# Second expert routing: sends to HBM two tiles at a place instead of four, routing steps moved to other places, and the first pass of maxima reduced two PSUM banks at a time

## The reference, cut to what matters

```python
x = L0_attn_x                                   # (8, 512, 128)
xn = _layernorm(x, axis=-1)
s = _L0_attn_ref(xn, ...)                       # two small attentions, a Holt filter, norms, a feed forward
g = _silu(_L0_ffn_ref(xn, Wg, w1, w2))          # top-1 of 16 experts
x = x + s * g
xn = _layernorm(x, axis=-1)
s = _L1_attn_ref(xn, Wq, Wk, Wv, Wo)            # causal, 16 heads, ALiBi
g = _silu(_L1_ffn_ref(xn, gate_w, gate_b, ...)) # top-2 of 8 experts
x = x + s * g
```

```python
logits = xt @ gate_w.T + gate_b
top_v, top_i = jax.lax.top_k(logits, TOP_K)     # TOP_K = 2, E = 8
w = jax.nn.softmax(top_v, axis=-1)
out = (w * sel).sum(axis=1)
```

## Time and profile before

| what | value |
|---|---|
| runs | 1189.53, 1193.96, 4205.56 us (median 1193.96) |
| the profiled execution's own time | 1191.96 us |
| its span | 1190.1 us |
| busy share of the span | PE 85%, VectorE 67%, ScalarE 54%, POOL 49% |
| mean granted TensorE clock | 0.92 |

### The profile page before, as it was taken

The page is one execution under the profiler, slowest core; times in us unless marked ns, Lnnn a source line. Parts: engine busy times, 40 slices in busy tenths (PEclk is TensorE's granted clock), DMA queues, the critical chain, the costliest instruction groups (busy, mean ns, idle before and its releaser), DMA issues. The chain is left out here.

```text
span 1190.1 us, 22919 instructions
## 1 busy us (share of the span) xinstructions
PE 1013.1 (85%) x7466; PEld 543.2 (46%) x7466; DVE 791.7 (67%) x2466; ACT 646.8 (54%) x1252; POOL 578.1 (49%) x670
## 2 busy tenths in 40 slices
PE   4878899999989898878788577777999899899797
PEld 2612279433434333323333244444889654445443
DVE  5597833678787888887765555765444477788641
ACT  1204732576667776656566344444444466677575
POOL 5276400337464655547677576743000155545564
PEclk8667999999999999988999787877999999999889
DMA  5853566733223232303324033233888644454321
GB/s 144 217 146 80 136 169 200 223 102 91 54 56 88 46 98 47 89 5 87 82 66 98 12 74 92 50 85 115 241 242 252 162 108 111 83 135 110 68 56 45
DMA packets 121864, 129.81 MB, mean 109 GB/s; under 512 B 13920, under 2 KB 104864, under 8 KB 121536
## 3 DMA queue, kind: packets, MB, share of 16 engines
q1 hardware_dynamic: 115184, 115.37, 37.4%
q0 software_dynamic: 6144, 12.60, 4.0%
q10 hardware_dynamic: 432, 0.52, 0.2%
HBM read 82.54 MB, written 52.35 MB: 113 GB/s over the span
## 5 line engine op out<-in xcount | busy, mean ns | idle before, releaser
L877 DVE TENSOR_REDUCE a_neg_max<-ps_banks 128x1 f32<-128x512 f32 x512 | 322.7, 681 | 74.5 <-PE ps_banks L590 66.4
L772 ACT ACTIVATE a_probs<-ps_banks 128x512 f32<-128x512 f32 x512 | 278.3, 599 | 143.1 <-PE ps_banks L583 138.4
L583 PE MATMUL ps_banks<-q_strip,k_strip 53*128 53x512 bf16 (+3 forms) x1024 | 281.0, 355 | 72.1 <-DVE a_neg_max L877 31.5
L590 PE MATMUL ps_banks<-k_strip,q_strip 51*128 51x512 bf16 (+3 forms) x1024 | 301.5, 363 | 24.5 <-DVE a_neg_max L883 11.8
L883 DVE CUSTOM_DVE_ANT_0 a_masked<-ps_banks,mask_wide 128x384 bf16<-128x384 f32 (+3 forms) x512 | 224.0, 487 | 90.3 <-PE ps_banks L590 74.6
L774 ACT ACTIVATE a_probs<-ps_banks 128x512 f32<-128x512 f32 x256 | 144.2, 600 | 81.2 <-PE ps_banks L541 72.1
L1067 POOL DMA_INDIRECT tokens<-made,at x96 | 93.6, 975 | 175.6 <-DMA made<-work 124.8
L583 PEld LDWEIGHTS ps_banks<-q_strip,k_strip 53*128 53x128 bf16 x1024 | 72.2, 95 | 161.9 <-issue 54.4
L624 PE MATMUL ps_banks<-a_probs,v_aug 128*32 128x512 f32 x1024 | 141.4, 625 | 0.5 <-ACT a_o_strip L779 0.2
L590 PEld LDWEIGHTS ps_banks<-k_strip,q_strip 51*128 51x128 bf16 x1024 | 74.4, 95 | 142.9 <-ACT a_probs L772 58.7
L2000 POOL DMA_INDIRECT sent<-xn,at x64 | 62.6, 978 | 54.7 <-DMA sent<-xn,at 24.4
(11 more groups left out here) (258 smaller groups left out, 1709.0 us busy)
## 6 DMA issues: line engine op xcount, KB each, us to landing
work<-in_pack SPq DMA_DIRECT2D x39, 450.0 KB, 3.5
q_rows<-a_q_parts SPq DMA_DIRECT2D x96, 128.0 KB
k_rows<-a_k_parts SPq DMA_DIRECT2D x96, 128.0 KB
q_strip<-q_rows SPq DMA_DIRECT2D x64, 192.0 KB
k_strip<-k_rows SPq DMA_DIRECT2D x64, 192.0 KB
work<-in_w SPq DMA_DIRECT2D x32, 256.0 KB, 3.1
sent<-in_zeros SPq DMA_DIRECT2D x14, 512.0 KB, 8.1
work<-sent SPq DMA_DIRECT2D x55, 128.0 KB, 3.3
```

Source lines behind the costliest of these rows:

```text
L583: mm = pe.matmul(sbank[:, at:at + hi - lo], k_now[rows(js, ROW_END), slot, kt * P:(kt + 1) * P], q_now[rows(js, ROW_END), slot, lo:hi], st ...
L590: mm = pe.matmul(mbank[:, at:at + hi - lo], q_next[rows(jm, ROW_SHIFT), slot, qt * P:(qt + 1) * P], k_next[rows(jm, ROW_SHIFT), slot, lo:h ...
L772: act.activation(probs[si // 4 % 2][:, si % 4, :], bank, ACT.Exp).then_inc(sems["probs"], 1)
L877: dve.tensor_reduce(neg_max[:, half, qt, hd:hd + 1], bank, AX.X, ALU.max, negate=True).then_inc(sems["max_out"], 1)
```

## The change

Four things are changed. (1) `routed` takes the three places of the ends as a list, so they can stand apart. (2) Group 0 in stage 5 gets its steps earlier and further apart: choose at 12, 14, 16, 18 (was 13, 15, 18, 21), count and scan at 20 (was 25), ends at 22, 24, 25 (was 27, 28, 29), slots at 27 (was 30), weights at 29 (was 28). (3) The sends stand two tiles at a place: at 0, 15, 19 and 24 of stage 6 (tiles 0 to 7), at 0, 14, 18 and 25 of stage 7 (8 to 15), at 0, 7, 17 and 23 of stage 8 (16 to 23), at 4 and 10 of stage 9 (24 to 27), and the last four tiles at 18 of stage 9 as before. The count of sends is unchanged: stages 6, 7, 8 and 9 have 8, 8, 8 and 8 tiles, where they had 12, 8, 4 and 8. (4) In the pass of maxima VectorE waits for two banks and reduces them in one instruction of 2 x 512 columns, and TensorE may be one pair ahead of what is reduced (`ahead = 2`, the four banks taken as two pairs).

```diff
 def routed(g, choose, count, ends, slots, weigh, table):
...
-                  *({ends + part: [("place", 0, (g, 1, part))]} for part in range(3)), {slots: [("place", 0, (g, 2))]}, {weigh: [("weigh", 0, g)]}, {table: [("place", 0, (g, 3))]})
+                  *({end: [("place", 0, (g, 1, part))]} for part, end in enumerate(ends)), {slots: [("place", 0, (g, 2))]}, {weigh: [("weigh", 0, g)]}, {table: [("place", 0, (g, 3))]})
...
-    NB - 2: sends(0, *4 * (0,), *4 * (13,), *4 * (30,)),
-    NB - 1: merged(routed(1, (12, 13, 15, 16), 18, 20, 23, 24, 26), sends(12, *4 * (17,), *4 * (30,))),
...
+    NB - 2: sends(0, *2 * (0,), *2 * (15,), *2 * (19,), *2 * (24,)),
+    NB - 1: merged(routed(1, (12, 13, 15, 16), 18, (20, 21, 22), 23, 24, 26), sends(8, *2 * (0,), *2 * (14,), *2 * (18,), *2 * (25,))),
...
+def paired(arg):
+
+    return arg[1] is not None and arg[0] is None
...
-        return {**({"scores": 1, "probs": 1} if arg[0] is not None else {}), **({"max_in": 1, "max_out": 1} if arg[1] is not None else {})}
+        return {**({"scores": 1, "probs": 1} if arg[0] is not None else {}), **({"max_in": 1, "max_out": 2 * (arg[1] % 2) if paired(arg) else 1} if arg[1] is not None else {})}
...
-                                mbank, ahead = banks[:, 2 + n.at("max_in") % 4, :], 3
+                                mbank, ahead = banks[:, 2 + n.at("max_in") % 4, :], 2
...
+                            if paired(arg):
+
+                                if mi % 2 == 1:
+                                    wait(dve, sems["max_in"], n.at("max_in") + 1)
+                                    both = banks[:, 1 + n.at("max_in") % 4:3 + n.at("max_in") % 4, :]
+                                    dve.tensor_reduce(neg_max[:, half, qt, QT + slot % QT::-QT], both, AX.X, ALU.max, negate=True).then_inc(sems["max_out"], 2)
+                            elif max_layer == 0:
```

More of the change, by code:

```diff
@@ L201 @@
     2: {24: [("masks", 0)]},
-    NB - 3: routed(0, (13, 15, 18, 21), 25, 27, 30, 28, 31),
-    NB - 2: sends(0, *4 * (0,), *4 * (13,), *4 * (30,)),
-    NB - 1: merged(routed(1, (12, 13, 15, 16), 18, 20, 23, 24, 26), sends(12, *4 * (17,), *4 * (30,))),
-    NB: merged(routed(2, (13, 14, 15, 16), 17, 20, 25, 26, 27), sends(20, *4 * (18,))),
-    ROUTE1: merged(routed(3, (8, 9, 10, 11), 13, 15, 18, 19, 21), sends(24, *4 * (4,)), sends(28, *4 * (18,))),
+    NB - 3: routed(0, (12, 14, 16, 18), 20, (22, 24, 25), 27, 29, 31),
+    NB - 2: sends(0, *2 * (0,), *2 * (15,), *2 * (19,), *2 * (24,)),
+    NB - 1: merged(routed(1, (12, 13, 15, 16), 18, (20, 21, 22), 23, 24, 26), sends(8, *2 * (0,), *2 * (14,), *2 * (18,), *2 * (25,))),
+    NB: merged(routed(2, (13, 14, 15, 16), 17, (20, 21, 22), 25, 26, 27), sends(16, *2 * (0,), *2 * (7,), *2 * (17,), *2 * (23,))),
+    ROUTE1: merged(routed(3, (8, 9, 10, 11), 13, (15, 16, 17), 18, 19, 21), sends(24, *2 * (4,), *2 * (10,)), sends(28, *4 * (18,))),
     **{MIX1 + i: mixed(-2, 8, 0, 18, 22, 24, 26, 28) for i in range(4)},
@@ L870, in _ @@
                             _, mi, max_layer = arg
-                            bank = banks[:, 2 + n.at("max_in") % 4 if b == -1 else MAX_BANK + n.at("max_in") % RING, :]
+                            bank = banks[:, MAX_BANK + n.at("max_in") % RING, :]
                             half, j, pieces = max_unit(mi, max_layer)
@@ L874, in _ @@
                             hd, e = QT * j + slot % QT, mi % 10
-                            wait(dve, sems["max_in"], n.at("max_in") + 1)
-                            if max_layer == 0:
+                            if paired(arg):
[4 more added lines that the diff above has]
+                            elif max_layer == 0:
+                                wait(dve, sems["max_in"], n.at("max_in") + 1)
                                 dve.tensor_reduce(neg_max[:, half, qt, hd:hd + 1], bank, AX.X, ALU.max, negate=True).then_inc(sems["max_out"], 1)
                             else:
+                                wait(dve, sems["max_in"], n.at("max_in") + 1)
                                 wait(dve, sems["max_out"], n.at("max_out") - 1)
```

## The result

| kernel | runs (us) | median |
|---|---|---|
| before | 1193.96, 1189.53, 4205.56, 1194.90 | 1194.43 |
| changed | 1175.42, 1177.87, 1176.26, 1170.73 | 1175.84 |

The ratio is 0.9851, with a 95% interval from 0.9802 to 0.9900 (the run at 4205.56 is left out of it). So some 18 us are gained: the interval is clear of no change and ends just short of a gain of 2%. The profiled executions are 1191.96 and 1175.42 us, 16.5 us apart.

A forecast was written before the change was run, and what follows sets the result against it. POOL's queue, with sends ahead of the scan of stage 7, was taken as the limit there. From 1191.96 us, -12.8 (stages 6 and 7), -4.9 (stage 8), -1.5 (stage 5) and -1.0 (maxima) gave 1172 us, range 1162 to 1186.

The forecast's parts named there:

- the forecast case: POOL's queue still sets the scan of stage 7: 1172 us, own range 1166 to 1178, chance 0.50.
- Stages 6 and 7: Fewer sends ahead on POOL: `ln3a` 5.9 us earlier plus 6.9 us ahead of the scan, gain 12.8 us.
- the second case: Rival: VectorE's wait in stage 7 goes altogether, by an earlier gather or rows landing sooner; 1165 us, chance 0.24.
- x2 at stage 7, 0.8 us late and covered: VectorE waits 0.8 us for x2 at the `ln3a`, which its three banks in hand cover.
- Stage 8: TensorE's 4.76 us wait to turn xn goes; net of delays and with a clock gain, 4.9 us less.
- the sign of being wrong: VectorE waiting over 3 us for x2 at the head of stage 7 or 8; 1 to 3 us was expected.
- the sends ahead of `ln2`: Sends at place 25 of stage 7 fall in POOL's 4.72 us idle time and cost about 2 us.
- both delays: In stage 8, later x2 and later y, from sends between the splits of q and k: 1.4 us charged together.
- the 1.5 us by clock: Stage 8, at mean clock 0.82, gains 1.5 us from a higher clock, out of 0 to 10.
- Stage 5: Group 0's routing moves from the stage's end to its middle: 1.5 us less, from -3.5 to +1.5.
- Pass of maxima: Reducing two banks at once, 1.12 us a pair against 1.20: 1.0 us less, from -2.5 to +4.
- The slower rival: Sends ahead of `ln2` in stages 6, 7 and 8 delay x2 by 6.8 us each: 1197.5 us, chance 0.06.

The follow-up runs named there:

- sends: The kernel before with only the new places of the sends in stages 6 to 9: 1150.4 us against 1175.4, ratio 0.9781.
- scan: The kernel before with two of the four tiles at place 17 of stage 7 sent at 21, behind the scan: 1189.8 us against 1195.1, ratio 0.9957.
- head: The kernel before with two of the four tiles at place 30 of stage 6 sent at 24, ahead of `ln2`: 1191.1 us against 1195.1, ratio 0.9973.
- after_b: The changed kernel, unchanged, timed again in the third group of runs: 1150.7 us against 1178.1 for the kernel before, ratio 0.9776.
- pairs: The kernel before with only the maxima reduced in pairs of banks: 1175.6 us against 1175.4, ratio 0.9993.
- after_again: The changed kernel, unchanged, timed again in the second group of runs: 1177.3 us against 1195.1 for the kernel before, ratio 0.9837.
- before_again: The kernel before, unchanged, timed again beside itself in the second group of runs: 1196.4 us against 1195.1, ratio 1.0008.
- late: The changed kernel without the sends at place 25 of stage 7, later tiles following two later each: 1154.9 us against 1178.1 for the kernel before, ratio 0.9802.
- group0: The kernel before with only group 0's steps in stage 5 at their new places: 1178.0 us against 1175.4, ratio 1.0023.
- single: The changed kernel with maxima reduced one bank at a time again, three banks ahead: 1149.9 us against 1175.4 for the kernel before, ratio 0.9782.
- single_b: The changed kernel with single-bank maxima again, repeated in the third group of runs: 1149.5 us against 1178.1 for the kernel before, ratio 0.9770.
- x2late: The changed kernel with two tiles moved from place 0 of stage 7 to place 24 of stage 6: 1157.3 us against 1178.1 for the kernel before, ratio 0.9839.

## Why the prediction was right, and where it was not

The forecast of 1172 us was 3.8 us under the median, and the mechanism is the one forecast: POOL's queue sets the scan of stage 7, and moving DMAs out from ahead of it shortens that stage. `sends` and `scan` show it in time and trace with one edit each, `head` in its trace alone. That the sum came out so near is in part luck. In the first pair of traces stages 5 to 8 are 20.2 us shorter, just the sum forecast, but only because the terms that missed made up for each other; the second pair has 17.0 us there, and `after_b` against `pairs` 27.3. And where the kernel before takes 1178 us (`after_b`, below), the same change gains 26 to 27 us, at the far end of the 14 to 26 that the 1166 to 1178 of the forecast case mean.

- **Stages 6 and 7: -12.8 forecast, -16.9 measured** in the first pair of traces, -16.3 in the second (134.8 in `after_again`, 151.1 in `before_again`). The steps on POOL came as worked out: the gate 2.6 us earlier (forecast 2.4), the `ln3a` 6.3 (5.9). The mis-sized term is the end of the scan, 16.2 instead of 12.8 earlier. I had kept the 5.12 us wait for the gathered rows and named its shortening only under the second case. It fell by 3.3 us, nearly all of the 3.4 that were missing, and left 1.15 us of VectorE's wait instead of 4. `head` shows the same fall (1.81), `scan` doesn't (4.92): it goes with the head start of the gather. Stage 7 also got its clock back: 0.91 before, 1.00 after, TensorE's busy time 58.76 and 56.52 us. I had put the gain in clock to stage 8.
- **x2 at stage 7, 0.8 us late and covered:** VectorE waits 0 us for it in the first trace and 1.6 in `after_again` and `after_b`. That is within the 1.8 us of three banks.
- **Stage 8: -4.9 forecast, -0.9 and -1.0 measured** on the chips of the first comparison and of `after_again`, but -6.7 in `after_b` against `pairs`, two traces of the other kind of chip (below). The wait to turn xn is gone, as forecast. In its place came what I named as the sign of being wrong, a wait of over 3 us for x2 (3.75 us, 4.0 in `after_again`, 3.8 in `after_b`). The step that failed here: I charged the sends ahead of `ln2` with 2 us, which is their 6.8 less the 4.72 us that POOL was idle there. But POOL waited there for VectorE's moments, and VectorE came late in part because the scan had held it for 14.53 us. With the scan early this cover shrinks: `late`, which has no sends there, is left with 2.59 us of it. The four sends take 5.35 us, and no landing is waited for, so `ln2` starts 3.0 us after the moments are there, and VectorE's wait for x2 grows by the same 3.0 (0.72 to 3.75). The larger part of the miss is in two other terms. I charged both delays with 1.4 us; TensorE's waits for maxima in stage 8 alone went from 5.0 to 8.4 us (6.4 to 8.3 in the second pair), and it waits 2.9 for `logits` or 2.4 for ScalarE on top. And the 1.5 us by clock aren't there: TensorE is busy 57.1 and 56.3 us in the first pair, 59.2 and 59.3 in the second, and the clock is 0.82 and 0.84, 0.81 and 0.80. `late` shows that the wait for x2 can be removed, but the time didn't fall with it.
- **Stage 5: -1.5 forecast.** -2.4 in the first pair, +0.4 in the second, -1.9 in `group0`. In `group0` stage 6 gave it back, and the kernel is not faster; `sends` without it is as fast as `single` with it. In the sum this term should have been 0.
- **Pass of maxima: -1.0 forecast, 0 measured** (`pairs`, and `after_b` against `single_b`). The work got shorter (65 ns for each instruction saved, 2.1 us for 32), and VectorE's new idle time behind TensorE's extra steps took it. The price of the reduction was nearly right, at 1.137 us where I had 1.12; that it would shorten the pass was not. The 125 ns for each instruction that the Trainium skill gives (page "Perfetto Trace Analysis", section "Optimizing Scalar/DVE Operations") are about twice the 65 ns that this trace shows, and neither reached the time.
- **The slower rival:** its mechanism is real. In `x2late` VectorE waits 6.9 us more where I had put 6.8 for a place with no slack, and the median is 6.5 us higher. It didn't decide because the three places of the change cost VectorE 0 to 1.6 us at the head of stage 7, 3.8 at stage 8, and none ahead of stage 9, where POOL still idles 3.95 us ahead of `ln2`.

What stays open: why the gain of stage 8 differs between the chips, and how much of each trace's stage lengths is the execution. Stages with the same code differ by several us from trace to trace: stage 6 takes 67.0 us in `after_b` and 71.4 in `late`, and in the same kernel (`single`, `single_b`) stage 7 takes 63.1 and 67.4 and stage 9, with the experts that follow it, 176.0 and 181.7. So the stage lengths say where the gain is, and the medians how large it is.

## What to carry to other kernels

Ask of a queue in order not only how much stands ahead of the step that others wait for, but what that step, once it is earlier, stops colliding with, and which idle stretch behind it closes. An idle gap read from the profile before is cover only as far as the change leaves its cause alone: here 4.72 us of it shrank to 2.59. And test each part of a bundle alone: one of four carried all of the gain here, and the shorter VectorE instruction and the shorter stage 5 gave their microseconds back at the next wait. And hold a trace against more than one trace of the base: two traces of one kernel can differ in a stage by more than the edit does.

## What the runs showed of the hardware

**A gather next to a bulk load.** In stage 7 SyncE issues four strip loads of 192 KB each, 34 to 39 us after the stage's start in ten of the fourteen traces, and 41 to 46 in the others. The first of them, in the kernel before and in the changed one:

```profile
642.13 0.33 SPq L494 DMA_DIRECT2D q_strip<-q_rows  x1
```
```profile
641.90 0.33 SPq L499 DMA_DIRECT2D q_strip<-q_rows  x1
```

The last of the gather's DMAs is issued at 643.63 before, 1.5 us behind this load, and at 640.09 after, 1.8 us ahead of it. All fourteen traces agree:

| first load, against the last DMA of the gather | POOL's wait for the rows (us) | traces |
|---|---|---|
| 1.5 and 1.2 us ahead of it | 5.12, 4.92 | before, `scan` |
| 0.1 us behind it | 4.59, 4.21, 4.53 | `before_again`, `pairs`, `group0` |
| 1.4 to 4.5 us behind it | 1.75 to 1.90 | the nine others |

No run moved the loads alone, so the collision is argued from this pattern.

**The same program differs by 1.4 to 1.7% between groups of runs.** The kernel before had medians of 1194.4 and 1195.1 us in two comparisons, 1175.4 and 1178.1 in two others. The last three were on three different chips; the chip of the first isn't on record, and no chip was tried twice, so that the chip makes the difference is the likely reading, not a shown one. The traces put most of it behind the start of stage 10, whatever the kernel: from there to the end it is 243 to 249 us in the six traces of the first kind, and 229 to 232 in the eight of the other. In stage 12 the clock is 1.00 and TensorE busy for 34.4 us in both `before_again` and `pairs`, but the stage takes 38.4 and 35.4 us. The rest is idle time of TensorE. The profile puts the longest piece of it, 2.1 us in `before_again`, down to ScalarE, which in turn had waited 3.1 us for TensorE, so these traces don't name the cause. The change is worth 1.5 to 1.6% on the one kind and 2.2% on the other.
